# One wait for row buffers per two chunks on GpSimd, in front of the even chunk

## What is computed

```python
# layer 0, per edge e with source src[e] and destination dst[e]
w5e = einsum(edge_feat16, W5[edge_type]) + b5[edge_type]
num = sum(h3[dst] * (h4[src] + w5e))            # softmax over one value
msg = score * (h2[src] + w5e)
x   = layernorm(x + h1 + segment_sum(msg, dst))
# layer 1
m   = relu(x[src] + edge_feat32 @ We + be) + 1e-7
a   = exp(m - segment_max(m)[dst]) / segment_sum(...)[dst]
x   = layernorm(x + (x + segment_sum(m * a, dst)) @ Wm + bm)
```

## Time and profile before

| | |
|---|---|
| median of 3 runs | 2188.85 us (2187.74 to 2201.08) |
| profiled execution | span 2193.7 us |
| stage 0, first chunk's scores to last | about 200 to 1160 us |
| stage 1 | about 1210 to 2130 us |
| TensorE busy | 1808.2 us (82%) |
| VectorE busy | 1649.8 us (75%) |
| ScalarE busy | 791.6 us (36%) |
| GpSimd busy | 1282.8 us (58%) |
| DMA | 321.30 MB, 146 GB/s over the span |

### The profile page before, as it was taken

How to read it: one execution, slowest core, us unless ns; L and a number is a source line. 1 busy time by engine, 2 the same in 40 slices (tenths; PEclk the granted TensorE clock), 3 DMA queues, 4 the chain that set the end, 5 groups by cost and what they waited for, 6 DMA issues and landing times.

```text
span 2193.7 us, 29535 instructions
## 1 busy us (share of the span) xinstructions
PE 1808.2 (82%) x9200; PEld 1086.3 (50%) x9200; DVE 1649.8 (75%) x3316; ACT 791.6 (36%) x1503; POOL 1282.8 (58%) x1347
## 2 busy tenths in 40 slices
PE   6599999999999999999981678788887878879863
PEld 5334555655555655555560245445444544545432
DVE  6534877878878788788787378778887877878876
ACT  3101223223322333223231145455554545545561
POOL 7365666666666666666614666666666666666624
PEclk9899999999999999999995789889998998989975
DMA  8933445554545555555442245555554545555541
GB/s 283 391 61 94 139 144 148 148 151 144 148 142 153 143 146 145 147 148 152 138 141 58 48 134 156 141 151 157 153 149 142 164 140 162 149 149 153 151 140 57
DMA packets 216065, 321.30 MB, mean 146 GB/s; under 512 B 61931, under 2 KB 123940, under 8 KB 215781
## 3 DMA queue, kind: packets, MB, share of 16 engines
q1 hardware_dynamic: 128950, 148.58, 23.3%
q0 software_dynamic: 43056, 68.05, 13.8%
q10 hardware_dynamic: 43904, 102.79, 13.1%
HBM read 186.00 MB, written 133.22 MB: 146 GB/s over the span
## 4 chain that ended last, share of the span: by engine, by line
PE 29%; issue 26%; DVE 16%; another core or an unknown queue 12%; ACT 11%; ACTq 3%; POOL 1%; DMA 1%; SPq 0%; DVEq 0%; POOLq 0%
PE wide L900 11%; PE wide L999 7%; DVE late L1210 3%; ACT block L819 3%; DVE edge_lists L1210 3%; DVE featm L1226 2%; DVE score L1216 2%; ACTq L812 2%; ACT prob_wide L796 2%; PE wide L1010 2%; ACT msg L797 1%; DVE h3d L1235 1%; ACT block L800 1%; PE wide L860 1%
## 5 line engine op out<-in xcount | busy, mean ns | idle before, releaser
L634 POOL DMA_INDIRECT rows<-d_x,idx x588 | 558.3, 950 | 342.1 <-issue 158.2
L624 POOL DMA_INDIRECT block<-d_h,idx x482 | 455.6, 945 | 278.8 <-issue 126.2
L900 PE MATMUL wide<-late,typed 125*128 125x512 bf16 (+1 forms) x936 | 282.4, 382 | 35.7 <-issue 35.3
L999 PE MATMUL wide<-late,ntype_i 125*128 125x512 bf16 x975 | 239.5, 403 | 53.9 <-DVE ntype_i L1346 49.7
L900 PE MATMUL wide<-edge_lists,typed 125*128 125x512 bf16 (+1 forms) x864 | 259.8, 381 | 22.1 <-issue 20.9
L1235 DVE TENSOR_TENSOR_SCAN h3d<-keep,h3d,bank 128x512 f32<-128x512 bf16 x98 | 125.4, 1280 | 176.4 <-issue 171.2
L999 PE MATMUL wide<-edge_lists,ntype_i 125*128 125x512 bf16 x936 | 223.4, 393 | 11.1 <-issue 11.0
L624 POOL DMA_INDIRECT rows<-d_h,idx x160 | 151.0, 944 | 132.7 <-remote 48.4
L1010 PE MATMUL wide<-ident,block 128*128 128x128 f32 x784 | 135.3, 319 | 93.6 <-ACT block L819 59.3
L999 PEld LDWEIGHTS wide<-late,ntype_i 125*128 125x128 bf16 x975 | 100.9, 104 | 175.9 <-DVE ntype_i L1346 50.1
L900 PE MATMUL wide<-late,ntype_i 125*128 125x512 bf16 (+1 forms) x468 | 179.0, 383 | 3.9 <-issue 3.5
(11 more groups left out here) (224 smaller groups left out, 3390.0 us busy)
## 6 DMA issues: line engine op xcount, KB each, us to landing
d_run<-block ACTq DMA_DIRECT2D x98, 512.0 KB
d_inj<-zeros SPq DMA_DIRECT2D x28, 896.0 KB
inj<-d_inj SPq DMA_DIRECT2D x98, 256.0 KB
d_run<-stage ACTq DMA_DIRECT2D x98, 256.0 KB
feat<-in_ea16x3T SPq DMA_DIRECT2D x196, 96.0 KB
types<-d_type SPq DMA_DIRECT2D x196, 64.0 KB
keep<-d_keep SPq DMA_DIRECT2D x196, 64.0 KB
keep<-d_pen SPq DMA_DIRECT2D x196, 64.0 KB
```

Of the source, the lines that this page charges most:

```text
L624: pool.indirect_dma_start(out=ring[c % RING][:, j, h, :], out_offset=None, in_=d_h24, in_offset=bass.IndirectOffsetOnAxis(ap=idx[:, c, at: ...
L634: pool.indirect_dma_start(out=rows1[c % RING1][:, j, h, :], out_offset=None, in_=d_x1, in_offset=bass.IndirectOffsetOnAxis(ap=idx[:, c, at ...
L900: ins = pe.matmul(p_pick[s][:, 0:cols], table0[n][:, k, :], hot0[b][:, k - b * KT, 0:cols], start=(k == 0 and n == 0), stop=(k == NT - 1 a ...
L999: ins = pe.matmul(p_hot[s], table[q][:, SPLIT * k:SPLIT * (k + 1), :].rearrange("p b c -> p (b c)"), hot[s][:, k, :], start=(k == 0 and q ...
```

## The change

GpSimd waits in front of even chunks only, then for both buffers of the pair: in stage 0 for `q2_ready` of chunks `c - 8` and `c - 7`, in stage 1 for `z_ready` of chunks `c - 4` and `c - 3`. The odd chunk's gathers follow without a wait. Nothing else differs.

```diff
@@ gather0
-                if c >= RING:
-                    pool.wait_ge(q2_ready[c % 2], (c - RING) // 2 + 1)
+                if c >= RING and c % 2 == 0:
+                    for s in range(2):
+                        pool.wait_ge(q2_ready[s], (c - RING) // 2 + 1)
@@ gather1
-                if c >= RING1:
-                    pool.wait_ge(z_ready[c % 2], (c - RING1) // 2 + 1)
+                if c >= RING1 and c % 2 == 0:
+                    for s in range(2):
+                        pool.wait_ge(z_ready[s], (c - RING1) // 2 + 1)
```

## The result

The changed kernel takes 2589.16 us (median of 3 runs, 2587.86 to 2597.11) against 2188.85 before: 1.182 of the time, 95% interval 1.177 to 1.187, some 400 us slower. The profiled execution has a span of 2595.3 us.

The account below looks back on a forecast made before the run. Bound: gathers hold TensorE's signals about 1.45 us a gather, then GpSimd restarts, TensorE almost as long. Span 2193.7 + 270 (stage 0) + 89 (stage 1) = 2553, median 4.9 lower: 2548 us, range 2340 to 2690.

Parts of the forecast that it names:

- A: Both stages: gathers hold TensorE's late signals until after the run, and TensorE stops; 2548 us, 2391 to 2686, chance 0.77.
- The release at 1.45 us a gather: Both stages: held signals are seen 17.4 us after the start of a run of 12, 20.3 for 14.
- What comes after the release in stage 0: Stage 0: TensorE's work left for the pair, 17.9 us less the 11.1 done before it stops: 6.8 us.
- the upper end of the range: TensorE's clock falls behind each stop, 1.5 us lost per pair, 92 pairs: 138 us more, 2686.
- The second wait "costs at most the 0.3 us that lie between any two gathers": Before even chunks: the added wait sits in GpSimd's sequencer and costs at most 0.3 us.
- Stage 1: Stage 1: pairs take 17.4 + 2.5 + 0.3 = 20.2 us against 18.3, times 47 pairs: +89 us.
- the case without a stop: Stage 1: if TensorE does not stop during the run, a pair takes 17.7 us, -28 us in all.
- TensorE's stop after 11.1 us: Both stages: TensorE works 11.1 us into a run, then stops; left are 6.8 us in stage 0, 2.5 in stage 1.
- The moved waits at nothing: Both stages: the even chunk starting one chunk later costs nothing, covered by rows gathered ahead; otherwise 9 us each time.
- The profile after: Signals in twos, GpSimd idle 7 us or more before even chunks only, its share near 50%, TensorE's near 70%.
- B: Rival: the hold opens inside a long run, so both chunks finish sooner; -53 us, 2136 us, chance 0.08.
- D: Rival: gathers only follow TensorE's own periods (8.93 of 9.97 us), the change is hidden; 2189 us within 1%, chance 0.08.

Follow-up runs that it names:

- u3: The kernel before with each chunk waiting for the signal of one chunk later, runs of 6 and 8 gathers kept: 2208.24 us, 1.000 of before.
- t4: The changed kernel plus a GpSimd wait, before each odd chunk's gathers, until the even chunk's rows have landed: 2315.88 us (one run), 1.057 of before.
- w7: The changed kernel with four GpSimd memsets between the even and odd chunk's gathers, on a chip with the hold: 2245.62 us, 1.023 of before.
- w12: The changed kernel with one GpSimd memset (128x330, about 0.4 us) behind each gather: 2178.65 us, 0.993 of before.
- w8: The changed kernel with stage 1's picking matmuls (512 columns) issued as two of 256, except each bank's first: 2750.06 us, 1.250 of before.
- v8: The changed kernel with each stage 1 picking matmul issued as two of 256, on the chip where before takes 1919.19 us: 1918.98 us, 0.9998.
- w11: The kernel before with one GpSimd memset (128x330, about 0.4 us) behind each gather: 2169.09 us, 0.987 of before.

## Why the prediction was right

Forecast 2548 us, range 2340 to 2690; measured 2589. The mechanism was the one named as A. That back-to-back gathers hold up TensorE's signals, and that this is the cost, is shown for the chips that have the hold: by the length of the run (u3: 1.000 with the later signal alone), by gaps (t4, w7) and by the pitch (w12). What the hold is made of is not shown. The traces do not tell either whether a finished matmul's signal is kept back or the matmul itself is done later than its row says, since a row's end is computed.

*The release at 1.45 us a gather* held. The 21 whole runs of 12 in stage 0 released 17.4 us after their start, in the mean, as forecast, and the runs of 14 after 20.1 (forecast 20.3), but for the two early ones above.

*What comes after the release in stage 0*, 6.8 us, was mis-sized. It took 7.3 in the mean behind runs of 12 and 7.1 behind runs of 14. The forecast had kept TensorE's clock out of it, and put it in the upper end of the range; the window behind the release has it at 0.78.

*The second wait "costs at most the 0.3 us that lie between any two gathers"* was the step that failed. From the signal's record to the first gather it is 0.26 us with one wait and 0.74 with two. ScalarE's rows, which start 0.02 to 0.03 us behind the signal, show it too: 0.71 from L724 at 674.23 to the gather at 674.94, 0.24 from 597.78 to 598.02. In the kernels with one stage changed it is 0.74 in that stage and 0.26 in the other. The sum had 0.3 for it in each pair; 0.44 x 92 is 40 us.

*Where the forecast fell short.* On the profiled span it is 43 us: 20 in stage 0, 13 in stage 1, 8 in front of stage 0's first waited gather and behind its last, for which the sum had no term, and 1 at the end. That the second wait alone comes to nearly the same number is luck. In stage 0 it is 20 us and the longer work after the release 18 (0.5 and 0.3 a pair); the releases of the runs of 14, two of them early, and a last pair with none behind it go the other way. Pairs took 25.4 and 27.7 us for 24.5 and 27.4.

*Stage 1*: +102 for +89, pairs of 20.5 for 20.2. They do not all take that: a tenth are under 18.4 and a tenth over 22.6, probably by how much of the second chunk TensorE had done when it stopped. No pair took the 17.7 of the case without a stop (the shortest 17.9).

*TensorE's stop after 11.1 us* was read from one run, and wrong as a rule, as w8 shows. It did no harm, since the mix of matmuls in a pair stayed.

*The moved waits at nothing* are shown by u3.

*The profile after* has what was forecast of GpSimd (50%, idle before even chunks alone) and of the signals in twos. TensorE was to be at about 70% and is at 78%: the forecast divided the old busy time by the new span, and the clock made the same matmuls 208 us longer.

*The rivals.* B (signals seen inside a long run) and D (the gathers only follow) are both false on the chip on which the forecast was measured, but for the two runs of 14 that opened early. The chip of v8 has B's sign, a signal seen 8.2 us into a run of 12, and D's steps and time: TensorE's 8.9 us, and a change that costs nothing. The forecast had no case for "it depends on the chip"; that the profile of before came from one with the hold is what carried it, and in this the forecast was lucky.

## What to carry to other kernels

Where gathers or other indirect DMAs of GpSimd run beside TensorE, hold the start of the instruction that needs TensorE's signal against the rows of the matmul that gives it, in and out of the gathers. If the signals come only behind a run, its length is a latency for every other engine: do not merge waits into longer runs, and let GpSimd issue a little slower (here 1.50 us apart was enough and 1.25 was not). Take the times on more than one chip, and if possible without the recording, before a wait or a pace is tuned to it.

## What the runs showed of the hardware

- On the chips where the kernel before takes 2189 to 2209 us, what TensorE signals late in a run of gathers at a pitch of 1.25 us is nearly always visible only behind the run. The medians from the run's start are 8.96 us for 6 gathers and 11.80 for 8 (before), 17.36 for 12 and 20.12 for 14 (after): 1.44 to 1.49 a gather. The gathers' own DMA packets do not slow down to that: the last one ends 2.2 to 2.6 us after the last gather's start in all four kinds of run, which is 0.2 us before the signal for 6 gathers and 1.5 before it for 14. So the moving of the rows alone does not set when the signals come.
- At a pitch of 1.5 us (w11, w12) there is no hold. On the fifth chip there is none at 1.25 either, and the kernel before takes 0.875 of the time.
- Of VectorE's and ScalarE's signals some get through where TensorE's of nearly the same time don't. In the run of 648.37 TensorE sees ScalarE's L711, which ended at 653.28, by 656.85 (L948), and VectorE's one-hot tiles, the last of which ended at 654.95, by 657.29 (L902), while its own `injT` of 655.48 is seen at 665.83. That one given later in a run gets through is not shown.
- TensorE goes on for about 60 matmuls after a run's start (59, 62 and 61 in the windows above, over 11.1, 7.6 and 7.6 us) and then in single steps. The timeline of the changed kernel in stage 1 shows one of 1.42 us; in w8, from 1744.04 on, the first are 0.71 apart:

```profile
1722.45 0.27 PE L989 MATMUL bank<-inj,merge 128*128 128x128 f32 x1 [0.62 <-issue]
1723.87 0.27 PE L989 MATMUL bank<-inj,merge 128*128 128x128 f32 x1 [1.15 <-issue]
1725.29 0.37 PE L989 MATMUL bank<-inj,merge 128*128 128x128 f32 x1 [1.16 <-issue]
```

  The Trainium skill (Advanced Engine Details and Errata, Engine Queue Depths) gives TensorE a queue of 64. The 59 to 62 matmuls lie near it; that it is this queue which fills up is argued and not shown.
- While TensorE stands, the DMA engines can be nearly idle, with a share of 0.16 in 659.50 to 665.80 against 0.58 in the 11 us before, or as busy as ever, with 0.60 in 1301.80 to 1308.10 before the change. So the hold does not go with how busy they are.
- Two semaphore waits in a row on GpSimd put the first gather 0.74 us behind the last signal, one wait 0.26, also where the other signal had come 7 us earlier.
